# Copying an expert tile's first-layer weights into fixed buffers on VectorE

## The reference, cut to what matters

```python
logits = x_flat @ gate_w.T
probs = softmax(logits)
top_w, sel = top_k(probs, 2)            # normalised to sum 1
h = gelu(einsum('th,ehf->tef', x_flat, W1) + b1)    # E=8, H=256, F=1024
y = einsum('tef,efh->teh', h, W2) + b2
out = einsum('teh,te->th', y, combine)
out = out + gelu(x_flat @ sW1 + sb1) @ sW2 + sb2
```

## Time and profile before

| what | value |
|---|---|
| runs | 3870.0, 3861.52, 3852.47 us; median 3861.52 us |
| span of the profiled execution | 3852.8 us |
| its own whole time | not listed; the runs lie between 3852.47 and 3870.0 us |
| busy: TensorE matmul / weight load | 3339.2 us (87%) / 2178.5 us (57%) |
| busy: VectorE / ScalarE / GpSimd | 2096.1 (54%) / 1512.5 (39%) / 628.1 us (16%) |
| expert tiles, first and last load of the owner | 1679.6 and 1957.6 us |

### The profile page before, as it was taken

The page is one execution under the profiler, slowest core; times in us unless marked ns, Lnnn a source line. Parts: engine busy times, 40 slices in busy tenths (PEclk is TensorE's granted clock), DMA queues, the critical chain, the costliest instruction groups (busy, mean ns, idle before and its releaser), DMA issues. The chain is left out here.

```text
span 3852.8 us, 110008 instructions
## 1 busy us (share of the span) xinstructions
PE 3339.2 (87%) x44394; PEld 2178.5 (57%) x44394; DVE 2096.1 (54%) x8237; ACT 1512.5 (39%) x4247; POOL 628.1 (16%) x361
## 2 busy tenths in 40 slices
PE   7894866989999965789984888999999999999899
PEld 3322542223232324678751444489999899999566
DVE  5324454555555516653328444467777677777554
ACT  3484542555555523666632222232222222222222
POOL 0000001666676730511100000000000000000000
PEclk8797987999999966899986999955555555555899
DMA  1000003000000033111120000100000000000000
GB/s 67 1 1 11 1 1 109 1 1 1 1 1 1 1 115 113 44 44 38 38 86 25 1 0 0 55 4 4 4 5 4 5 5 4 5 4 5 6 7 10
DMA packets 53380, 79.51 MB, mean 21 GB/s; under 512 B 11878, under 2 KB 43323, under 8 KB 51996
## 3 DMA queue, kind: packets, MB, share of 16 engines
q1 hardware_dynamic: 47504, 61.59, 4.9%
q0 software_dynamic: 3408, 9.34, 0.7%
q10 hardware_dynamic: 1988, 1.77, 0.1%
HBM read 56.01 MB, written 16.67 MB: 19 GB/s over the span
## 5 line engine op out<-in xcount | busy, mean ns | idle before, releaser
L1308 DVE TENSOR_REDUCE diff_mx<-diff_m_ps 128x1 f32<-128x512 f32 x512 | 329.8, 686 | 330.3 <-PE diff_m_ps L1158 330.3
L2753 PE MATMUL gru_sums<-gru_take,gru_u 128*128 128x4 f16 x12288 | 478.4, 167 | 4.9 <-issue 4.1
L2753 PE MATMUL gru_sums<-gru_keep,gru_u 128*128 128x4 f16 x12288 | 470.9, 166 | 5.2 <-DVE gru_keep L2827 3.5
L2753 PEld LDWEIGHTS gru_sums<-gru_take,gru_u 128*128 128x128 f16 x12288 | 431.2, 105 | 5.1 <-issue 4.2
L2753 PEld LDWEIGHTS gru_sums<-gru_keep,gru_u 128*128 128x128 f16 x12288 | 410.0, 104 | 21.4 <-issue 5.8
L1262 ACT ACTIVATE diff_probs<-diff_s_ps 128x512 f32<-128x512 f32 x512 | 277.9, 595 | 222.2 <-PE diff_s_ps L1152 222.1
L1152 PE MATMUL diff_s_ps<-diff_qk 32*128 32x512 f32 x1024 | 292.6, 645 | 63.6 <-DVE diff_mx L1308 56.0
L2753 PE MATMUL gru_sums<-gru_rh,gru_u 128*128 128x4 f16 x6144 | 278.3, 170 | 26.1 <-DVE gru_rh L2822 4.2
L1158 PE MATMUL diff_m_ps<-diff_qk 32*128 32x512 f32 x1024 | 293.7, 650 | 6.4 <-DVE diff_mx L1308 6.4
L1354 POOL TENSOR_TENSOR diff_sums<-diff_sums,diff_probs 128x2048 f32<-128x2048 f32 x64 | 289.3, 4520 | 31.5 <-ACT diff_probs L1262 31.2
L2753 PEld LDWEIGHTS gru_sums<-gru_rh,gru_u 128*128 128x128 f16 x6144 | 235.7, 106 | 68.7 <-DVE gru_rh L2822 4.9
(11 more groups left out here) (486 smaller groups left out, 5757.8 us busy)
## 6 DMA issues: line engine op xcount, KB each, us to landing
moe_weights<-in_L_ffn_W SPq DMA_DIRECT2D x16, 1024.0 KB, 13.1
expert_slots<-diff_blank SPq DMA_DIRECT2D x1, 5031.0 KB, 22.6
stream_a<-expert_slots SPq DMA_DIRECT2D x39, 129.0 KB, 2.0
moe_weights<-in_L_cond_w_R SPq DMA_DIRECT2D x1, 4096.0 KB, 15.0
moe_both<-expert_pairs SPq DMA_DIRECT2D x4, 1024.0 KB, 9.6
stream_b<-in_x SPq DMA_DIRECT2D x4, 512.0 KB, 7.9
hyp_wf<-in_L_cond_w_f SPq DMA_DIRECT2D x2, 1024.0 KB, 8.6
stream_b<-in_xT SPq DMA_DIRECT2D x1, 2048.0 KB, 12.3
```

The source lines that it names most:

```text
L1308: dve.tensor_reduce(mx[:, i % 2, kt, at:at + 1], m_ps[:, m % 3, :], X_AXIS, ALU.max).then_inc(ph.maxes_ready, 1)
L2753: last = pe.matmul(sums[:, par, g, m * B:(m + 1) * B], part[:, g, c, m * P:(m + 1) * P], state[:, c * B:(c + 1) * B], start=False, stop=(l ...
```

## The change

VectorE gets a new step, copy_first_layer(n): it loads the owner of tile n into a register of its own and copies both fp16 parts of that expert's first layer (2 x 2048 values for each partition) into one of two fixed buffers, by the parity of n. The buffers are slot 8, free once the last expert's raw weights have been used: the first half for even tiles, the second for odd ones. copy_first_layer(NT) stands at the end of iteration NT - 1, behind part2 of the last expert's first layer; copy_first_layer(n+1) stands in iteration n behind second_half(n+1), and at n = NT behind a wait for part2 of the second layer. From tile NT + 2 on, the step waits until hidden(n-2) has been multiplied. TensorE waits for the copy (first_copied) and reads the first layer at an address known when the program is built; it still loads the owner, with which the second layer is addressed.

```diff
--- before.py
+++ after.py
@@ -1646,12 +1646,12 @@
          ph.turned, ph.ranked, ph.tops_found, ph.tops_turned, ph.tops_reduced, ph.tops_spread, ph.scales_ready,
          ph.part1_ready, ph.part2_ready, ph.goals_ready, ph.meta_set, ph.rows_ready, ph.rows_copied, ph.x_turned,
          ph.x1_ready, ph.x2_ready, ph.hidden_ready, ph.gelu_done, ph.h1_ready, ph.h2_ready, ph.out_ready,
-         ph.out_taken, ph.tiles_known, ph.product_made, ph.table_ready) = ph.semaphores(
+         ph.out_taken, ph.tiles_known, ph.product_made, ph.table_ready, ph.first_copied) = ph.semaphores(
             "dve_step", "asked", "answered", "made", "gates_ready",
             "turned", "ranked", "tops_found", "tops_turned", "tops_reduced", "tops_spread", "scales_ready",
             "part1_ready", "part2_ready", "goals_ready", "meta_set", "rows_ready", "rows_copied", "x_turned",
             "x1_ready", "x2_ready", "hidden_ready", "gelu_done", "h1_ready", "h2_ready", "out_ready", "out_taken",
-            "tiles_known", "product_made", "table_ready")
+            "tiles_known", "product_made", "table_ready", "first_copied")
         in_flight = Phase(nc, ctx, "moe_dma")
         flags = in_flight.semaphores(*(f"weights_loaded_{x}" for x in range(EARLY, E + 1)), *(f"tile_loaded_{k}" for k in range(4)))
         ph.weights_loaded, ph.tile_loaded = dict(zip(range(EARLY, E + 1), flags)), flags[E + 1 - EARLY:]
@@ -1668,6 +1668,8 @@
             return inner.enter_context(nc.sbuf_tensor("moe_" + name, shape, dt))
 
         raw, parts, halves = experts.raw, experts.parts, experts.halves
+        by_slot = experts.halves.rearrange("p s (k l n) -> p s k l n", k=2, l=2)
+        first_layers = shaped(experts.halves[:, E, :], 2, 2, W_HALF)
         table = sb("table", [P, SLOT_TILES, LOWS])
         lows, wg = experts.lows, experts.wg
         owner = sb("owner", [P, SLOT_TILES], I32)
@@ -1829,8 +1831,8 @@
                             pe.wait_ge(ph.part2_ready, 2 * (E - EARLY) + 1)
                             pe.wait_ge(ph.tiles_known, 1)
                         home[n % 2] = pe.value_load(owner[0:1, n - NT:n - NT + 1], min_val=0, max_val=E - 1)
-                        hidden(n, lambda pw, at, size: halves[:, bass.ds(home[n % 2], 1), 2 * pw * W_HALF + at:2 * pw * W_HALF + at + size
-                                                              ].squeeze(1))
+                        pe.wait_ge(ph.first_copied, n - NT + 1)
+                        hidden(n, lambda pw, at, size: first_layers[:, n % 2, pw, at:at + size])
                     if n == 1:
                         pe.wait_ge(ph.made, 2)
                         pe.wait_ge(ph.ranked, 1)
@@ -1961,6 +1963,14 @@
                                              in1=xparts[:, n % 2, 0, :, :], op0=ALU.mult, op1=ALU.subtract
                                              ).then_inc(ph.x2_ready, 1)
 
+                def copy_first_layer(n):
+
+                    if n >= NT + 2:
+                        dve.wait_ge(ph.hidden_ready, 2 * (n - 1))
+                    slot = dve.value_load(owner[0:1, n - NT:n - NT + 1], min_val=0, max_val=E - 1)
+                    dve.tensor_copy(first_layers[:, n % 2, :, :], by_slot[:, bass.ds(slot, 1), :, 0, :].squeeze(1)
+                                    ).then_inc(ph.first_copied, 1)
+
                 def take_out(n):
                     dve.wait_ge(ph.out_ready, n + 1)
                     if n < NT:
@@ -2058,6 +2068,10 @@
                         part2(EARLY + SCALED_AT.index(n - 1), 0)
                     if n == NT:
                         part2(E, 1)
+                    if NT <= n < ALL - 1:
+                        if n == NT:
+                            dve.wait_ge(ph.part2_ready, 2 * (E - EARLY) + 2)
+                        copy_first_layer(n + 1)
                     if n in SCALED_AT:
                         reduce_tops(SCALED_AT.index(n) + 1, 2)
                     if n < ALL:
@@ -2078,6 +2092,8 @@
                         part2(EARLY + SCALED_AT.index(n - 1), 1)
                     if n == NT - 1:
                         part2(E, 0)
+                        dve.wait_ge(ph.part2_ready, 2 * (E - EARLY) + 1)
+                        copy_first_layer(NT)
 
             @block.gpsimd
             def _(pool):
```

## The result

The changed kernel takes 3836.01 us in the median of 20 runs (3820.99 to 3860.34), the kernel before 3865.76 us in the 20 runs beside them (3846.78 to 3886.2). The ratio is 0.9929, 95% interval 0.9908 to 0.9949: 20 to 36 us less, where 30 us were forecast. The forecast was 3832 us in a range of 3804 to 3868.

The account below looks back on a forecast made before the run. TensorE's register operations in the expert tiles' first layer bound the 7.38 us period; the memory loop would then set 6.56. 36 periods x (7.38 - 6.56) + 0.8 = 30 us; 3861.5 - 30 = 3832 us, range 3804 to 3868.

Parts of the forecast that it names:

- What bound before, and what was removed: Expert tiles' first layer on TensorE: 32 register operations a tile bind; removing them saves 1.61 us of the 7.38 us period.
- TensorE's own bound: Expert tiles: without the register operations TensorE alone would need 5.77 us a tile.
- What is late next: Expert tiles: loop of output taking, scatter, load into the same buffer and turn; 13.0 us over two periods, 6.56 taken.
- The hold of the copy: GpSimd's scatter, issued 0.35 us ahead of VectorE's copy, isn't held by it; cost put at nothing.
- the first rival: The copy holds the scatter's descriptors 1.2 us in the expert tiles; period 7.1 + 0.06 us, 3853 us; chance 0.24.
- The copy's place: On VectorE the copy starts about 1.15 us after the output's taking: 0.45 to second_half, 0.7 for the register load.
- The clock: TensorE's granted clock stays at 1.00 in the expert tiles, though TensorE would idle some 0.4 us a period.
- the prediction's own signs: Right: scatters 0.96 us, taking to load 3.2 us. Wrong: granted clock leaving 1.00 between 1680 and 1930 us.
- The sum: 36 periods x (7.38 - 6.56) + 0.8 at the last tile = 30 us saved, giving 3832 us.
- The slower case: A long copy holds the scatter; from 1.8 us of holding the kernel slows, 3871 to 3914 us; chance 0.12.

## Why the prediction was right, and where its steps were off

**What bound before, and what was removed: right.** The first layer's weight loads took 2.7 us instead of 4.28, also without any copy, and eight buffers in the kernel before changed nothing. So TensorE with its addresses in registers bound it, and not the loop. TensorE's own bound was put at 5.77 us and is 5.52: I kept the 0.50 us from the turn to the first layer, but once the register operations are gone the sequencer runs ahead and the step takes 0.22.

**What is late next: right, and the heart of it.** The load's wait for the scatter is what TensorE waits for, and the experiments with three, five and eight buffers move the period as the loop says. Its terms in the timeline of the changed kernel: turn to first layer 0.73 (I had 0.88), to the first GELU 1.63 (1.71), to the second L1908 3.69 (3.68), to the taking 1.42 (1.42); taking to load 3.24 where no copy hits the scatter (3.23), load to landing 2.1 in the median (2.1 with the handover). Together 12.8 us, 6.4 a period; 6.64 was measured without a copy, so variation of scatters and loads adds 0.2, where I had added 0.06.

**The hold of the copy: the step that failed.** The prediction put it at nothing, "by these rows", because a scatter that was 0.18 us ahead of a VectorE operation lasted only 1.09 us. That operation had two inputs; the plain copy behaves in another way. In the changed kernel 22 of 39 scatters were hit. When the copy began 0.03 us after the scatter, the scatter lasted 1.38 us (16 times), at 0.12 to 0.13 us 1.46 to 1.48, at 0.25 us 1.59, at 0.35 to 0.36 us 1.70 to 1.71. Each ended 0.12 us after the copy's end. Five copies that began 0.54 to 0.86 us after it left it at 0.96. So the mechanism of the first rival holds, in part of the tiles, at 0.42 us (0.75 at most) and not the 1.2 us that the rival had: the remaining work of the scatter isn't added to the hold, only waits for its end. No scatter here began behind a copy, so what a copy that already runs does isn't shown. The period, 6.90 us, lies about midway between the forecast's 6.56 and that rival's 7.16.

It also works the other way round. Of the five copies, the three that began 0.54, 0.60 and 0.67 us after a scatter lasted 1.45, 1.39 and 1.31 us and all ended 1.99 us after the scatter's start; from 0.81 us on a copy takes its 1.23 us:

```profile
1927.05 0.96 POOL L2134 DMA_INDIRECT expert_pairs<-stream_a  x1 [4.74 <-DVE stream_a L1985]
1927.59 1.45 DVE L1971 COPY moe_weights<-moe_weights 128x4096 f16 x1 [0.25 <-issue]
```

In the kernel with the second copy the two sides lie closer together: one 0.52 us behind the scatter was itself held (1.47 us), one 0.48 us behind still held it (1.83 us):

```profile
1721.27 0.96 POOL L2138 DMA_INDIRECT expert_pairs<-stream_a  x1 [4.73 <-DVE stream_a L1989]
1721.79 1.47 DVE L1974 COPY stream_a<-moe_weights 128x4096 f16 x1 [0.28 <-issue]
...
1873.47 1.83 POOL L2138 DMA_INDIRECT expert_pairs<-stream_a  x1 [6.67 <-DVE stream_a L1989]
1873.96 1.23 DVE L1974 COPY stream_a<-moe_weights 128x4096 f16 x1 [0.27 <-issue]
```

So each can keep the other out, and what counted here was whether the copy began before about 0.5 us of the scatter were over.

The Trainium skill (SBUF — State Buffer, Who interferes with whom) has the copy hold back descriptor writing until its end, and the same page, A bandwidth-pool intuition that's wrong (but worth ruling out), puts the end of the block about 115 ns behind the copy; the trace agrees with 0.12 us. The page also says that whichever instruction starts first keeps the other out for its whole length. By that the scatter, 0.35 us ahead in the forecast, would have held the copy, so the prediction's sentence that the page leads to the first rival doesn't follow. The trace agrees for copies that began 0.54 to 0.67 us after the scatter. Up to 0.36 us the scatter started first and was held by the later copy, which was not delayed (1.23 us); the measurement decides.

**The copy's place.** I put it 1.15 us behind the taking; it came at 0.85 when nothing else held it, since the register load, 0.30 + 0.19 us, ran beside second_half (copy 0.40 us after its start). That is why most copies began right on the scatter.

**The clock: kept at 1.00, it fell three times in the 35 steady periods** (at 1793.7, 1834.7 and 1913.2 us) and once in the last tile, each time to 1.2 GHz. By the prediction's own signs that was a miss, as were the scatters, not at 0.96, and the way from taking to load, 3.66 us in the median and not 3.2. Before each fall TensorE had waited 1.8 to 2.6 us at the turn and again 0.5 before the first layer, but a wait of 2.6 us at 1849.5 wasn't followed by one; what decides isn't shown. The second fall (timeline and then window of the changed kernel):

```profile
1833.80 0.44 PE L1771 MATMUL moe_x_ps<-ident,stream_a 128*128 128x128 f32 x2 [1.48 <-DMA stream_a<-expert_slots]
```

```profile
1834.70:1838.10 3.40, 3.40 (x35) 3.40 (x34) 1.71 (x2) 0.84 (x4) 0.92 (x1) 0.51 0.13 43
```

The weight loads of the tile's first layer, begun at 1834.52, end at 1838.84: 4.3 us instead of 2.7, so a fall costs 1.6 us. Some waits thus cost more than their length; three falls over 35 tiles are at most 0.14 us a tile, a part of the 6.90 against 6.63.

**The sum.** 6.90 instead of 6.56 us a tile gives 17 us over 36 tiles; the stage as profiled has 18.4: 0.6 from the second to the fourth turn (I had nothing), 16.5 in the 35 periods, 1.4 behind the last turn (0.8). The prediction had 30. The median fell by 30 all the same. A part of that is the front: sorted, the 20 runs before lie ten up to 3861.5 and ten from 3870.0 us, the 20 after eleven up to 3837.6 and nine from 3845.2. The means of the lower ones differ by 24.4 us and those of the upper by 24.7. If these are the two ways of the front, about 5 of the 30 us are their mixture; for every kernel with four runs or more the profiled one lies on the side where this would put it. The gap between 24 and the stage's 18 us stays open: there is one profile for each kernel, and the stretches that the edits leave nearly alone, from the first L1152 to the second tile's turn and behind the stage, each differ by 8 to 9 us among the ten profiles. That the time came out at 3836, 4 us from the forecast, with a step worth 12 us missing, is luck.

**The slower case** needed a copy that holds the scatter for over 1.8 us. The copy takes 1.23 us, as the bytes of the fp32 copy said, and even two in a row don't hold it longer.

## What to carry to other kernels

Before taking work off the engine that binds, write down the next loop with its buffers: the time from the use of a buffer to its next use, over the number of periods that it may span. Here 13.3 us over two periods stood at 6.6 us, just below the 7.38 that was visible, and hid nearly three quarters of the gain (18 of 69 us in the stage remained); one more buffer gave it back. Where a VectorE copy may meet a scatter that somebody waits for, start it well over 0.5 us later or make it wait; at 0.54 to 0.67 us the scatter was free of it and the copy up to 0.22 us longer.

## What the runs showed of the hardware that I had not expected

A plain fp16 copy on VectorE (4096 values a partition, 1.23 us) holds a GpSimd scatter that began up to 0.48 us before it, until 0.12 us after the copy's end. A scatter that began 0.52 to 0.67 us before the copy keeps its 0.96 us and holds the copy, which then ends 1.99 us after the scatter's start. With two copies that follow each other without a gap the scatter still ends 0.12 us after the first. The front of this program runs in one of two ways, 25 us apart and with a mean granted clock of 0.83 to 0.84 or 0.80 in the first 652 us, whichever kernel follows; what picks the way stays open.
